# Recommendation tower on one core: steps 0 and 1 in halves, a store on ScalarE, GpSimd's queue and the last tile's MLP in another order

## The reference

```
xk = x0
for W in (W0, W1, W2):                                   # (32, hk_1, 64)
    xk = relu(einsum('bmd,bhd,mhk->bkd', x0, xk, W))     # every field times every row of xk
    outs.append(sum(xk, axis=2))
h = concatenate([concatenate(outs, 1), dense_ctx], 1)
h = maximum(h @ W_top1 + b_top1, 0)                      # 208 -> 512
h = maximum(h @ W_top2 + b_top2, 0)                      # 512 -> 256
y = h @ W_top3
```

## Time and profile before

| | |
|---|---|
| median of 3 runs | 1182.02 us (1181.14 to 1182.32) |
| the profiled execution: time, span | 1184.45 us, 1182.6 us |
| busy in the span | PE 1118.4, DVE 1111.5, ACT 835.7, POOL 917.6 us |
| DMA | 167.32 MB, mean 141 GB/s |
| two turns in the middle | 69.05 us (DVE's step 28 begins at 1009.85, step 30 at 1078.91) |

### The profile page before, as it was taken

How to read it: one execution, slowest core, us unless ns; L and a number is a source line. 1 busy time by engine, 2 the same in 40 slices (tenths; PEclk the granted TensorE clock), 3 DMA queues, 4 the chain that set the end, 5 groups by cost and what they waited for, 6 DMA issues and landing times.

```text
span 1182.6 us, 15683 instructions
## 1 busy us (share of the span) xinstructions
PE 1118.4 (95%) x5312; PEld 395.6 (33%) x5312; DVE 1111.5 (94%) x509; ACT 835.7 (71%) x2385; POOL 917.6 (78%) x640
## 2 busy tenths in 40 slices
PE   0587999999999999999999999999999999999997
PEld 0122233333333333333333333333333333333343
DVE  0598999999999999999999999999999999999994
ACT  0466577677868777686877778687767868777782
POOL 6767888888888888888888888888888888884400
PEclk9898999999999999999999999999999999999998
DMA  4895788767768876666887666788766668876200
GB/s 110 227 185 116 154 166 173 151 135 146 146 130 164 173 160 143 134 140 135 161 173 158 139 135 137 142 161 173 155 141 137 141 136 161 174 152 146 47 1 1
DMA packets 76480, 167.32 MB, mean 141 GB/s; under 512 B 22032, under 2 KB 39328, under 8 KB 76400
## 3 DMA queue, kind: packets, MB, share of 16 engines
q1 hardware_dynamic: 58704, 159.59, 64.0%
q0 software_dynamic: 16384, 4.23, 3.6%
q10 hardware_dynamic: 1312, 2.50, 0.8%
HBM read 157.86 MB, written 8.40 MB: 141 GB/s over the span
## 4 chain that ended last, share of the span: by engine, by line
PE 83%; DMA 6%; POOL 5%; issue 2%; ACT 1%; SPq 1%; ACTq 1%; DVE 0%; POOLq 0%; DVEq 0%
PE acc L643 77%; DMA q_tile<-x_of_steps 4%; POOL x_rows L260 4%; PE acc L716 3%; POOL p_l L272 2%; DMA x_rows<-in_table,ids_s 1%; PE acc L702 1%; PE acc L704 1%; DMA x_of_steps<-x_rows 1%; PE acc L724 1%; SPq L197 1%; ACTq L477 0%; SPq L225 0%; ACT xb L324 0%; ACT h L448 0%
## 5 line engine op out<-in xcount | busy, mean ns | idle before, releaser
L643 PE MATMUL acc<-p_dve,w_s 128*64 128x512 f32 x3840 | 855.9, 595 | 15.7 <-DVE p_dve L557 14.8
L260 POOL DMA_INDIRECT x_rows<-in_table,ids_s x512 | 491.8, 961 | 147.2 <-issue 130.9
L557 DVE TENSOR_TENSOR p_dve<-spread,xb 128x3072 f32<-128x3072 f32 (+2 forms) x224 | 566.1, 2585 | 4.7 <-issue 3.3
L557 DVE TENSOR_TENSOR p_dve<-spread,xa 128x2048 f32<-128x2048 f32 (+1 forms) x192 | 495.6, 2636 | 13.7 <-ACT xa L315 5.7
L643 PEld LDWEIGHTS acc<-p_dve,w_s 128*64 128x64 f32 x3840 | 271.2, 137 | 552.5 <-issue 486.8
L324 ACT ACTIVATE xb<-acc 32x512 f32<-32x512 f32 x512 | 288.8, 564 | 22.2 <-DVE p_dve L557 15.6
L272 POOL TENSOR_TENSOR p_l<-spread,q_tile 128x2048 f32<-128x2048 f32 x60 | 273.0, 4574 | 16.1 <-DMA q_tile<-x_of_steps 14.2
L315 ACT ACTIVATE xa<-acc 64x512 f32<-64x512 f32 x256 | 145.9, 570 | 152.7 <-PE acc L643 123.5
L283 POOL TENSOR_TENSOR p_pool<-spread,x_s 128x1024 f32<-128x1024 f32 x64 | 152.6, 2385 | 78.6 <-PE acc L643 37.3
L643 PE MATMUL acc<-p_l,w_s 128*64 128x512 f32 (+1 forms) x640 | 153.2, 613 | 38.5 <-ACT p_l L342 36.3
L333 ACT ACTIVATE x_s<-acc 64x512 f32<-64x512 f32 x256 | 151.6, 592 | 10.7 <-ACT y_row L467 4.8
(11 more groups left out here) (20 smaller groups left out, 202.9 us busy)
## 6 DMA issues: line engine op xcount, KB each, us to landing
spread<-x_of_steps SPq DMA_DIRECT2D x246, 512.0 KB, 17.5
q_tile<-x_of_steps SPq DMA_DIRECT2D x126, 128.0 KB, 11.4
x_rows<-in_table,ids_s POOLq DMA_INDIRECT x512
x_of_steps<-x_rows SPq DMA_DIRECT2D x64, 128.0 KB
spread<-x_of_steps SPq DMA_DIRECT2D x24, 128.0 KB, 4.3
w_s<-in_w SPq DMA_DIRECT2D x2, 512.0 KB, 6.4
spread<-x_of_steps ACTq DMA_DIRECT2D x8, 128.0 KB, 5.6
spread<-x_of_steps ACTq DMA_DIRECT2D x2, 512.0 KB, 12.2
```

The costliest lines, as they stand in the source:

```text
L260: nc.gpsimd.indirect_dma_start(out=x_rows[:, s % 2, i * DIM:(i + 1) * DIM], out_offset=None, in_=table, in_offset=bass.IndirectOffsetOnAxi ...
L557: nc.vector.tensor_tensor(p_dve[:, to:to + n, :], spread[:, s % 3, tile:tile + n, :], over(x[:], n), ALU.mult).then_inc(dve_made, n)
L643: last = nc.tensor.matmul(acc[b * K:(b + 1) * K, :], w, prod[:, b * BLK:(b + 1) * BLK], start=start, stop=stop)
```

## The change

Its parts:
- Columns of block b are no longer b*512 to b*512+511 but, in each half of 512 columns, the b-th 256 (`of_block`). So every matmul reads its columns in two pieces and each ReLU writes two; `halves` does the same for the accumulator's side, and the host reorders the ids of steps 0 and 1.
- Steps 0 and 1: gathers, stores, loads, squares, first-layer products and the contraction of layer 0 in two halves of 512 columns. The second half of step 1 is stored by ScalarE; half of that half's loads and of step 1's b tiles are issued there too. Layer 0 of step 1 stands behind chunks 10 and 13.
- `keep_busy`: matmuls without use of their result, two and four around step 0's second half, two and one at the end.
- GpSimd: no wait for x1a_ready; four gathers between `product(0, 1)` and `product(1, 1)`; `product(0, 2)` directly behind the first-layer products of step 2, of which GpSimd makes chunks 2 and 3 and VectorE 0 and 1. p_pool of step 0 is contracted in turn 1 behind chunk 4.
- Sums of layer 0 in steps 1 and 3 by VectorE. q of step 2 is loaded ahead of its a tiles.
- End: MLP1 of tile 14 behind chunk 4 for 10, MLP2 behind 15 for 14, MLP3 behind 6 for 3; z of tile 14 moved ahead of x2_b in turn 31; out_2(30) ahead of x2_b(31); VectorE's last group of two as one and one.

The core of the diff (context and repeated forms cut):

```diff
+GROUPS_LAST = [(0, 2), (2, 3), (5, 2), (8, 3), (11, 1), (12, 2), (14, 1), (15, 1)]
-POOL_AFTER_OF_0 = 14
+POOL_AFTER_L1_OF_0, POOL_AFTER_L2_OF_0 = 4, 14
-L0_OF_1_AFTER = 10
-L0_OF_2_AFTER = 9
+L0_OF_1_AFTER = 10, 13
+L0_OF_2_AFTER = 7
-GATHERED_IN_TURN_0 = 56
-LATE_MLP1_AFTER, LATE_MLP2_AFTER, LATE_MLP3_AFTER = 10, 14, 3
+BUSY_BETWEEN, BUSY_BEHIND = 2, 4
+BUSY_AT_END = 2, 1
+LATE_MLP1_AFTER, LATE_MLP2_AFTER, LATE_MLP3_AFTER = 4, 15, 6
+def sums_by_act(s):
+    return s % 2 == 1 and s >= 5
+def of_block(x, b):
+    return x.rearrange("p (h b n) -> p b h n", h=2, b=2)[:, b]
+def halves(acc):
+    return acc.rearrange("p (h n) -> p h n", h=2)
...
         def _(sp):
-            store_x(0)
-            sp.wait_ge(x_stored, 32)
-            load_q(0)
-            load_a(0)
-            load_b(0)
-            store_x(1)
...
+            for b in range(2):
+                store_half_by(sp, 0, b, x_stored)
+                sp.wait_ge(x_stored, 32 * (b + 1))
+                load_half(0, b, SP_QUADS)
+            load_b(0, SP_QUADS)
+            store_half_by(sp, 1, 0, x_stored)
+            sp.wait_ge(x_stored, 96)
+            q_is_free(1)
+            load_half(1, 0, ALL_QUADS)
+            sp.wait_ge(half_stored_by_act, 32)
+            load_half(1, 1, SP_QUADS)
+            load_b(1, SP_QUADS)
...
         def _(pool):
-                for c in 0, 2:
+                for c in (0, 2) if s > 2 else (2,):
...
-            gathers(0, 2 * XI)
-            pool.wait_ge(x1a_ready, 1)
-            gathers(2 * XI, 3 * XI)
+            gathers(0, 3 * XI)
             product(0, 1)
+            gathers(3 * XI, 3 * XI + THEN)
             product(1, 1)
-            gathers(3 * XI, GATHERED_IN_TURN_0)
+            gathers(3 * XI + THEN, gathers_before(1))
             for s in range(1, STEPS):
...
-                gathers(n if s > 1 else GATHERED_IN_TURN_0, n + THEN)
+                if s > 1:
+                    gathers(n, n + THEN)
                 product(s - 1, 2)
...
         def _(act):
+                if s == 0:
+                    store_half_by(act, 1, 1, half_stored_by_act)
+                    half_squares(1, 0)
+                    act.wait_ge(half_stored_by_act, 32)
+                    load_half_by(act, 1, 1, ACT_QUADS)
+                    load_tiles_by(act, 1, NA, NT - NA, ACT_QUADS, b_loaded[1])
+                    half_squares(1, 1)
...
         def _(dve):
-            first_layer_products(0)
+            first_layer_half(0, 0, 0, CP)
+            first_layer_half(0, 1, 0, CP // 2)
+            first_layer_half(0, 1, CP // 2, CP // 2)
...
+                        if s == 1 and c == L0_OF_2_AFTER + 1:
+                            first_layer_of_2()
...
         def _(pe):
-                    last = nc.tensor.matmul(acc[b * K:(b + 1) * K, :], w,
-                                            prod[:, b * BLK:(b + 1) * BLK], start=start, stop=stop)
+                    last = nc.tensor.matmul(halves(acc[b * K:(b + 1) * K, :]), w, of_block(prod, b),
+                                            start=start, stop=stop)
...
+            def keep_busy(acc, n):
+                for _ in range(n):
+                    nc.tensor.matmul(acc[0:K, :], w1_s[:, 0, :],
+                                     wt2[:, 0:BLK // H2, :].rearrange("p k n -> p (k n)"), start=True, stop=True)
...
-            layer0(0, 0)
+            layer0_half(0, 0)
+            keep_busy(acc2, BUSY_BETWEEN)
+            layer0_half(0, 1)
+            keep_busy(acc2, BUSY_BEHIND)
...
+            pe.wait_ge(out_ready[1], STEPS)
+            keep_busy(acc1[0], BUSY_AT_END[0])
             mlp1(TILES - 1)
+            keep_busy(acc1[0], BUSY_AT_END[1])
             mlp2(TILES - 1)
             mlp3(TILES - 1)
```

More of the change, by code:

```diff
@@ L141, in build_kernel @@
         x_stored = sem("x_stored")
+        half_stored_by_act = sem("half_stored_by_act")
         q_loaded = sem("q_loaded")
-        tile_loaded = [[sem(f"tile{i}_of_step{s}_loaded") for i in range(NA - 1)] for s in range(2)]
+        half_gathered = [[sem(f"half{b}_of_step{s}_gathered") for b in range(2)] for s in range(2)]
+        half_q_loaded = [[sem(f"half{b}_of_step{s}_q_loaded") for b in range(2)] for s in range(2)]
+        half_a_loaded = [[sem(f"half{b}_of_step{s}_a_loaded") for b in range(2)] for s in range(2)]
         a_loaded = [sem(f"a_loaded{u}") for u in range(3)]
@@ L189, in store_x, with load_half @@
                     sp.dma_start(dst, x_rows[:, s % 2, :]).then_inc(x_stored, 16)
[L191 to L198, removed]
+            def load_half(s, b, quads):
+                load_half_by(sp, s, b, quads)
             def load_a(s):
@@ L203, in load_a, with load_b @@
                     sp.wait_ge(dve_made, dve_from(s - 3, 2) + A_USED)
[L204 to L212, removed]
+                sp.wait_ge(x_stored, stored(s))
+                load_tiles_by(sp, s, 0, NA, ALL_QUADS, a_loaded[s % 3])
+            def load_b(s, quads):
                 if s >= 3:
@@ L661, in layer0 @@
-                    contract(acc0, w0_s[0:rows, c, :], p_l0[0:rows, c, :], c == CP, c == CP - 1
-                             ).then_inc(l0_used, 1)
+                    if c == CP:
+                        pe.wait_ge(squares_made, 2 * (s + 1))
+                    elif s == 2 and c < CP // 2:
+                        pe.wait_ge(l0_made_by_dve, l0_by_dve(2))
+                    else:
+                        pe.wait_ge(l0_made, l0_by_pool(s) - CP + c + 1)
+                    last = contract(acc0, w0_s[0:rows, c, :], p_l0[0:rows, c, :], c == CP, c == CP - 1)
@@ new lines, in layer0, with layer0_half @@
+                last.then_inc(l0_used, 2)
+            def layer0_half(s, h):
+                if s > 0 and h == 0:
+                    pe.wait_ge(x1b_ready, s)
+                    pe.wait_ge(out_ready[0], s)
+                for c in CP, *range(CP):
+                    rows = P if c < CP else FIELDS
+                    if c == CP:
+                        pe.wait_ge(squares_made, 2 * s + h + 1)
+                    else:
+                        pe.wait_ge(l0_made_by_dve, 2 * CP * s + CP * h + c + 1)
+                    for b in range(2):
+                        last = nc.tensor.matmul(halves(acc0[b * K:(b + 1) * K, :])[:, h], w0_s[0:rows, c, :],
+                                                of_block(p_l0[0:rows, c, :], b)[:, h],
+                                                start=c == CP, stop=c == CP - 1)
+                last.then_inc(l0_used, 1)
```

228 lines of the change are left out of this document (143 added, 85 removed).

## The result

The changed kernel takes 1179.68 us, median of 16 runs (1176.01 to 1183.82), beside 1183.51 of the kernel before on the same chip (16 runs, 1181.14 to 1185.94): ratio 0.9969, 95% interval 0.9958 to 0.9980. The medians are 3.8 us apart; the forecast was 8.4. The profiled execution took 1183.16 us, with a span of 1181.4 against 1182.6.

A forecast was written before the change was run, and what follows sets the result against it. TensorE was taken as the bound, without a gap from 205 to 1154 us, so only ramp and end count. Ramp 5.4 (1.3 + 4.7 - 0.6) plus end 3.0 gave 8.4 us: 1173.6 us, 8-in-10 range 1167.5 to 1180.

The forecast's parts named there:

- Turns 0 and 1: Ramp's first part: halves start step 0's next layer 4 to 8 us sooner, but product(0,1) shifts by 0.
- the cap: Turn 1's second part on VectorE hangs on product(0,1) behind 48 gathers, so the halves' gained time becomes idle.
- Held gathers: Turns 0 and 1: gathers wait for VectorE's first-layer instructions, 3 to 6 us in all.
- the loads: Steps 0 and 1: loading in 2 KB pieces for 4 KB costs 0, at most 3 us.
- the slack that I had named: VectorE's first part of turn 1 could start 7 us later than expected without delaying its second part at 78.93.
- Turn 1 to 2: VectorE takes two first-layer chunks of step 2: a 2.2 us instruction replaces 3.51 us of idle, 1.3 us won.
- Rival A: Port lock: GpSimd holds up VectorE's new instruction 2.4 or up to 4.55 us; gain 3.5 to 6 us, chance 0.14.
- Turns 2 to 4: GpSimd's earlier product(0,2) and step 3 gathers remove five VectorE stalls, 4.7 us, less 0.6 for a reduction.
- four gathers 76.1, product(1,1) 78.5: GpSimd's list in turn 1: these end times, then eight gathers to 88.6 and the first-layer instruction to 93.1.
- The middle: Matmuls reading columns in two pieces from 205 to 1154 us cost TensorE 0.
- Rival C: Middle: reading in pieces slows TensorE; at 3% the kernel takes 1200 us; chance 0.11.
- The end: Last steps: 0.7 us from a removed TensorE wait, 2.4 from the clock staying up, less 0.1: 3.0 us.

The follow-up runs named there:

- nb: The changed kernel without the six keep_busy filler matmuls around step 0's second half: 0.9952 (0.9934 to 0.9970) of the kernel before.
- p0g2: The changed kernel with GpSimd's step 0 chunk contracted behind chunk 0 and GpSimd making all four first-layer products of step 2: 1175.62 us, 0.9940.

## Why the forecast was off

**Turns 0 and 1: the cap held.** product(0,1) began at 68.97 (forecast 68.7 within 2), x_b(1) at 74.41, VectorE's second part at 79.09 against 78.93. Held gathers were there again: five that together took 5.4 us too long, inside the 3 to 6 of the forecast. But I expected 3 to 5 us of idle time ahead of that part and it was 0.31: the loads cost more than the 0 that I took. ScalarE's half store took 6.3 us to land, the second half's tiles were used at 61.44 and 65.57, and x_a(1) came at 68.04, so VectorE's first part started at 70.44, 7 us later than I thought. That used up just the slack that I had named.

**Turn 1 to 2: the step that failed.** The sum had VectorE's new instruction at 2.2 us; it took 6.6. The lock was Rival A, priced at 2.4 or 4.55 us and given 0.14; it cost 4.4, the remainder of two GpSimd instructions in a row. I had argued against it that the first-layer product would be over at 93.1. That came from the list of the next paragraph. Even with that list in time VectorE is first by some 0.5 us only: its instruction starts at 95.70, and the `x_s` that product(0,2) waits for is there at about 96.2.

**Turns 2 to 4: where it began.** The step that failed at the root is the list "four gathers 76.1, product(1,1) 78.5": it puts the wait for TensorE at nothing, and that wait was 4.59 us. p_pool is a single buffer, and the diff moved its contraction from behind chunk 14 of turn 0 to behind chunk 4 of turn 1. Behind chunk 0 the list runs as I wrote it (product(1,1) at 76.45), and the ramp gives 5.15 us of 5.4. As it is, the stalls 0.98, 1.14 and 1.76 us have gone, 0.47 has become 2.87 and 0.32 stays, one reduction (0.6) is added, and step 2 starts 3.2 us later: the ramp is 2.05 us longer, for 5.4 us shorter in the forecast.

**The middle.** 0, as taken; Rival C is refuted by the windows. (Its price was counted low: 2410 records in 500 us are some 2290 pairs from 205 to 1154 us, not 2050, so 3% would be 29 us and not 26.)

**The end.** 3.0 us forecast, 3.2 in the profiled pair, 1.4 in medians. Against the old end with its clock up, the terms come out as written: 0.7 for the wait and the rest of the order (0.8 measured), 2.4 for the clock (69.07 less 66.6). VectorE's 1.2 us of waiting for x_b of step 31 was 1.09. What was mis-sized is the 2.4: it was read from one execution and carried to the median in full, and the clock fell in two of four.

**The sum.** The profiled pair differ by 1.3 us in time, the medians by 3.8. The changed kernel's executions vary by 7.8 us, and the times go with the granted clock: the five longest (1181.29 to 1183.82 us) have a mean of 0.991 to 0.993, the eleven others (1176.01 to 1179.97) of 0.994 to 0.999. The profiled one is one of the five (0.993), so the ramp's loss of 2.05 us is that of a long execution (beside one of the kernel before that is above its median too, 1184.45 us). How much of it is the stall at 146.29, absent in nb, wasn't resolved. The measured 3.8 us lies in Rival A's 3.5 to 6, but not by Rival A's sum, which leaves the ramp a gain of 0.5 us or more (3.5 less the end's 3.0): A had the lock, and not the late list behind it. The early contraction is, with p0g2, the best of the kernels measured: 7.0 us below the kernel before, and stable (1174.55 to 1176.61). Where x_a(0) is held it needs the wait at the 32nd gather too, and then only equals the kernel before (1.0011); that kernel wasn't timed on a chip without the hold.

## What to carry to other kernels

When an edit moves the reader of a single buffer to a later place on its own engine, follow the writer's list to its end: here 4.6 us of one wait became 4.4 of a port lock and 3 of a late load, on three engines. VectorE instructions with both inputs in SBUF and GpSimd's long ones should be kept apart in time by a margin larger than the lateness that GpSimd's list can pick up; with one input in PSUM they ran side by side here. And a clock dip seen in one profile is a chance, not a term: look for it in a second execution before it enters a sum.

## Not expected of the hardware

- The port lock holds over two GpSimd instructions in a row: 2048 elements on VectorE took 6.27 to 8.31 us for 2.29 in the six profiles where GpSimd had its two to do just then (each time it ended 2.2 us behind GpSimd's second), and GpSimd's 1024 elements 3.99 us for 2.37 where VectorE had. The Trainium skill ("SBUF — State Buffer", Who interferes with whom) has whoever issues first keep the port for the instruction; the rows agree, and show that the loser doesn't get it between the winner's two.
- A gather is held too: 2.85 us for 0.94 at 100.08, beside VectorE's first-layer instruction, which ended at 102.08. From 200 to 1000 us, beside VectorE's products with an input in PSUM, every gather took 0.94 to 0.98.
- A matmul operand read in two pieces of 1 KB costs the same as one of 2 KB, to 0.01 us in 500.
- On three chips of the five, ScalarE or VectorE go on up to 32 us after the TensorE records that they wait for, beside unbroken gathers, and the same change that gains 0.3 to 0.4% on two chips loses 2.1% on one of the three. A verdict from one chip would not have held for the others.
- The clock fell behind an idle time of 1.97 us of TensorE in two of four executions with the same waits, and not at the same record.
